# A windowed-attention network on one Trainium2 core: another order of TensorE's blocks in a slot

## The reference

```
def attn_layer(x, Wqkv, qs, ksc, Wo):          # x: 4 x 512 x 128, its second half of channels shifted by a token
    q, k, v = split(x @ Wqkv, 3)               # 1024 columns each
    q = rotary(l2norm(q) * qs)                 # with tables that depend on the position
    k = rotary(l2norm(k) * ksc)
    # a window of 32 queries sees its own 32 keys and the 32 before, masked to a band
    sim = einsum('bhwie,bhwje->bhwij', q, look_back(k)) * 8
    out = einsum('bhwij,bhwje->bhwie', softmax(sim), look_back(v))
    return out.reshape(b, n, 1024) @ Wo

def ffn_layer(x, g, bln, W1, b1, W2, b2):      # layer norm, 128 -> 2 x 341 -> 128
    a, gate = split(layernorm(x, g, bln) @ W1 + b1, 2)
    return a * gelu(gate) @ W2 + b2
```

## Time and profile before

| | |
|---|---|
| median of 3 runs | 1823.83 us (1823.41 to 1828.24) |
| the profiled execution | 1824.23 us, span 1822.2 us |
| granted TensorE clock, mean | 0.992 |
| PE busy | 1750.3 us, 96% |
| PEld busy | 1116.2 us, 61% |
| DVE busy | 1619.0 us, 89% |
| ACT busy | 1327.5 us, 73% |
| POOL busy | 1500.4 us, 82% |
| DMA | 16 engines 25.1% busy with the one queue |

### The profile page before, as it was taken

How to read it: one execution, slowest core, us unless ns; L and a number is a source line. 1 busy time by engine, 2 the same in 40 slices (tenths; PEclk the granted TensorE clock), 3 DMA queues, 4 the chain that set the end, 5 groups by cost and what they waited for, 6 DMA issues and landing times.

```text
span 1822.2 us, 48666 instructions
## 1 busy us (share of the span) xinstructions
PE 1750.3 (96%) x18122; PEld 1116.2 (61%) x18122; DVE 1619.0 (89%) x2782; ACT 1327.5 (73%) x2362; POOL 1500.4 (82%) x1204
## 2 busy tenths in 40 slices
PE   7699999999999999999999999999999999999986
PEld 6356666666666666666666666666666666666663
DVE  7799998999999989989999999899999998988874
ACT  3577877877778778778777777787776877877763
POOL 4799888888888888988888888888888888888860
PEclk9999999999999999999999999999999999999998
DMA  4132222222222222322223222222222222222221
GB/s 114 28 87 67 68 71 57 60 73 76 71 63 69 63 66 71 76 65 68 63 56 81 72 70 72 54 63 73 75 72 62 68 58 58 59 71 56 56 64 29
DMA packets 155273, 120.59 MB, mean 66 GB/s; under 512 B 42607, under 2 KB 151457, under 8 KB 154913
## 3 DMA queue, kind: packets, MB, share of 16 engines
q1 hardware_dynamic: 155041, 117.48, 25.1%
HBM read 18.79 MB, written 1.05 MB: 11 GB/s over the span
## 4 chain that ended last, share of the span: by engine, by line
PE 77%; DVE 13%; POOL 5%; issue 3%; SPq 1%; ACT 1%; DMA 1%; DVEq 0%; POOLq 0%; ACTq 0%
PE qk_bank L376 17%; PE ring_bank L448 10%; PE ring_bank L472 9%; PE ring_bank L389 8%; PE sc_bank L423 7%; PE ring_bank L516 6%; PE ring_bank L436 4%; PE ring_bank L399 3%; PE ring_bank L527 3%; PE ring_bank L461 3%; PE ring_bank L410 3%; DVE rn L842 2%; DVE step L837 2%; DVE o L898 2%; DVE qkn L858 2%
## 5 line engine op out<-in xcount | busy, mean ns | idle before, releaser
L1053 POOL TENSOR_TENSOR turned<-qkn,tables 128x512 f32<-128x512 f32 x384 | 489.3, 1274 | 209.8 <-DVE qkn L850 201.5
L1060 POOL TENSOR_TENSOR turned<-qkn,tables 128x512 f32<-128x512 f32 x384 | 496.7, 1294 | 0.0
L376 PE MATMUL qk_bank<-wqkv,xT 128*128 128x512 f32 x768 | 366.5, 600 | 18.8 <-DVE qkn L858 18.6
L1089 POOL TENSOR_TENSOR turned<-turned 128x512 f32<-128x512 f32 x192 | 255.0, 1328 | 15.1
L1096 POOL TENSOR_TENSOR turned<-turned 128x512 f32<-128x512 f32 x192 | 245.1, 1277 | 15.1
L448 PEld LDWEIGHTS ring_bank<-vw,pT 128*32 128x32 f32 x6144 | 156.6, 110 | 143.8 <-issue 143.7
L654 ACT ACTIVATE kB<-ring_bank 64x512 f32<-64x512 f32 x384 | 225.3, 587 | 23.5 <-PE ring_bank L410 21.2
L824 DVE TENSOR_REDUCE ss<-sq 128x16 f32<-128x1024 f32 x192 | 232.0, 1208 | 6.8 <-ACT sq L618 6.8
L627 ACT ACTIVATE vs<-ring_bank 128x512 f32<-128x512 f32 x192 | 114.7, 598 | 163.1 <-PE ring_bank L389 153.4
L898 DVE TENSOR_TENSOR o<-ring_bank,rr 128x512 f32<-128x512 f32 x192 | 132.1, 688 | 104.2 <-PE ring_bank L448 101.3
L389 PE MATMUL ring_bank<-wqkv,xT 128*128 128x512 f32 x384 | 216.1, 645 | 1.6 <-DVE x L978 1.6
(11 more groups left out here) (169 smaller groups left out, 3129.3 us busy)
## 6 DMA issues: line engine op xcount, KB each, us to landing
vw<-vs SPq DMA_DIRECT2D x1152, 64.0 KB, 2.1
vw<-vs SPq DMA_DIRECT2D x672, 32.0 KB, 1.9
wqkv<-in_L_ffn_Wqkv_dram SPq DMA_DIRECT2D x20, 384.0 KB, 3.5
wo<-in_L_ffn_Wo_dram SPq DMA_DIRECT2D x20, 128.0 KB, 3.3
w<-in_L_ffn_W_dram SPq DMA_DIRECT2D x6, 341.0 KB, 3.4
wqkv<-in_L_ffn_Wqkv_dram SPq DMA_DIRECT2D x1, 1536.0 KB, 9.5
x<-in_x_dram SPq DMA_DIRECT2D x2, 512.0 KB, 4.7
out_dram<-x SPq DMA_DIRECT2D x4, 256.0 KB, 2.3
```

Source lines behind the costliest of these rows:

```text
L376: mm = pe.matmul(QK[u % 2][:, i * UW:(i + 1) * UW], tok, wqkv[:, layer % 2, cut:cut + UW], start=True, stop=True)
L1053: return pool.tensor_tensor(heads(turned[:, u % 2, 2 * i, :]), heads(qkn[:, u % 2, i * UW:(i + 1) * UW]), table.unsqueeze(1).to_broadcast( ...
L1060: return pool.tensor_tensor(halves(turned[:, u % 2, 2 * i + 1, :]), halves(qkn[:, u % 2, i * UW:(i + 1) * UW])[:, :, ::-1, :], table.rearr ...
L1089: pool.tensor_tensor(q, q, turned[:, u % 2, 1, :], ALU.add).then_inc(q_summed, 1)
```

## The change

In PE's loop the v projection moves from behind attend to directly behind the q and k projections, and the turning of o moves behind the scores, so that attend and scores stand side by side. DVE's finish moves ahead of centre in the slots with s=1; it has work for the last four groups alone. The turns of the ring follow PE's order: v, pv, o, p in a slot where it was pv, v, o, p.

```diff
@@ PE's loop @@
             for n in range(SLOTS):
                 g, s = n // UPG, n % UPG
                 queries_keys(n)
+                values(n)
                 attend(n - 5)
-                values(n)
+                scores(n - 3)
                 transpose_o(n - 6)
-                scores(n - 3)
                 transpose_p(n - 4)
@@ DVE's loop @@
                 invert_sum(n - 5)
                 less_maxima(n - 4)
                 if s == 1:
+                    finish(g - 3)
                     centre(g - 2)
...
                 scale_o(n - 5)
                 if s == 3:
                     layer_norm(g - 2)
-                if s == 1:
-                    finish(g - 3)
```

## The result

The changed kernel takes 1871.97 us in the median (1871.19 to 1872.79, 4 runs) against 1823.62 for the kernel before: a ratio of 1.026, 95% interval 1.0242 to 1.0278, or 48 us slower. The profiled execution has a span of 1870.8 us.

What follows compares the result with a forecast made beforehand. PE was taken to bound most slots, with DVE needing 92% of the same time. Slot terms gave +1.11 a group, +24.4 over 22 groups, plus 1.4 for finish: 1824.23 becomes 1850, range 1812 to 1886.

Steps and rivals of the forecast that it cites:

- PE's saving: TensorE's slot: joining attend and scores leaves one tiling entry and exit of four, saving 0.37 us per slot.
- the 71 us: Upper limit of PE's saving: 0.37 in each of 192 slots, reached only if nothing else binds.
- DVE's loop and the lock: DVE: later attend delays scale_o; Newton steps wait for POOL products; slot 1 +0.26, slots 2 and 3 +0.95.
- the folded bias: PE work in slot 2 of one group in four, taking up most of the delay: 0.76 on average.
- ACT's chain: ACT runs oT, squares, pT; later o delays pT, holding q transposes: slot 0 +0.50, slot 4 +0.40.
- the four short slots: Slots 0, 1, 4 and 5 of a group, forecast at +0.50, +0.26, +0.40 and -0.27.
- Slots 6 and 7 are long ..., so PE's saving counts: ... -0.54: Slots 6 and 7: 19.53 less 2 x 0.37, plus 0.1 each for a bank held by oT: -0.54.
- 22 steady groups give +24.4: Whole run: the sum of +1.11 a group was counted over 22 steady groups, giving +24.4 us.
- the third rival: Lock missed in every slot: cycle 8.7 in slots 0, 1, 4, 5; +3.6 a group, 1903 us; chance 0.12.
- The first: Rival: DVE running ahead absorbs the longer loop, so only tiling savings count; 1753 or 1791 us; chance 0.14.
- The second: Rival: Newton steps of slots 2 and 3 slip through, pT costs half; 1828 us, within 0.3%; chance 0.10.
- If that cover goes, p waits for the v eviction some 0.2 a slot: ACT's v copy waits for later window DMAs; if later o stops covering this, p waits 0.2 a slot.

Runs made afterwards that it cites:

- both cuts and the seventh buffer: Changed kernel with ACT squaring before it copies o, POOL's q sum cut to 8 columns, and a seventh v buffer: 1781.82 us, ratio 0.9755.
- v_alone: Changed kernel with o put back ahead of the scores, so only v moves ahead of attend: 1867.2 us, ratio 1.0223.
- after_short_sum: Changed kernel with POOL's sum for q cut to 8 of 512 columns: 1821.61 us, 0.9969 of the kernel before.
- before_short_sum: Kernel before with POOL's sum for q cut to 8 of 512 columns: 1788.94 us, ratio 0.9791.
- join_early: Kernel before with the scores moved directly behind attend, ahead of v and o, attend staying in place: 1855.01 us, ratio 1.0151.
- o_alone: Kernel before with only the o transposes moved behind the scores: 1868.42 us, ratio 1.0232.
- squares_first: Changed kernel with ACT squaring q and k before it copies the turned o: 1869.74 us, ratio 1.0242.
- attend_first: Kernel before with attend moved ahead of the q and k projections: 1806.11 us, ratio 0.9891.

## Why the prediction was right

I forecast 1850 in a range of 1812 to 1886; 1872 lies in it, on the side and by the mechanism forecast, but the change cost 48 us and not 26. It stands at the very end of the forecast's own range of 1832 to 1872, so the mechanism was right and the size was not.

**PE's saving.** Forecast 0.37 a slot with the step from attend to scores at 0.83. It is 0.90 (929.82 - 928.92), so the step itself is 0.10, between its ends of 0.03 and 0.21 and nearer to the lower: the two blocks do join. The saving is 0.30 where nothing waits, as in slot 0 with both cuts and the seventh buffer (7.23 for 7.55). The cost of a change of tiling is there in the blocks (0.09 in, 0.18 out), as the drain that the Trainium skill (TensorEngine Tiling (Array Packing), Key Properties) gives to it would have it. But the 71 us were out of reach: 0.30 in 192 slots is 58, and even with three chains shortened the groups won 0.79 each and not 2.4.

**DVE's loop and the lock.** Right in place and size: scale_o forecast at 3.92, measured 3.92; slot 1 forecast at 8.4, measured 8.30; slots 2 and 3 +0.95, measured +1.02, and with the folded bias +0.76, measured +0.69 over groups 2 to 22. v_alone shows the cause, after_short_sum against before_short_sum the link through POOL's product. join_early shows that the link does not need a late attend. That the small DVE step and the POOL product exclude each other, as the Trainium skill says (SBUF — State Buffer, SBUF: two separate sides), fits the ends 0.04 apart and the 0.17 of the step without it.

**ACT's chain.** Slots 0 and 4 forecast at 8.05 and 7.95, measured 7.86 both. pT's end was forecast at 7.33 and measured at 7.31; the q transposes followed it by 0.06 where I had allowed more. o_alone and squares_first show the cause.

**What was mis-sized.** Over groups 2 to 22 the four short slots gave +0.94 (forecast +0.89) and slots 2 and 3 +0.69 (+0.76), so it was not there. Two terms were. First, "Slots 6 and 7 are long ..., so PE's saving counts: ... -0.54": they gave 0.18 in group 12. Slot 6 gave 0.20 and slot 7 nothing. The new order of turns puts attend's bank behind that of the output projection, so attend in slots 3 and 7 waits for the residual addition. In slot 7 (982.46) DVE ends it at 985.21, and attend starts at 985.32, 2.86 into the slot and not 2.67:

```profile
984.79 0.42 DVE L908 TENSOR_TENSOR xT<-xT,ring_bank 64x256 f32<-64x256 f32 x1
```

```profile
985.32 1.08 PE L448 MATMUL ring_bank<-vw,pT 128*32 128x128 f32 x32
986.19 1.08 PE L423 MATMUL sc_bank<-kB,qT 128*32 128x128 f32 x32
```

The join is dearer than taken, by 0.07 in slot 1 and 0.04 here (0.87 between the two rows), and the down projection, which waits for oT's bank, loses 0.15 in all where I had taken 0.1. Over the 21 groups these two slots miss the forecast by 7.7 us. Second, "22 steady groups give +24.4" left out groups 0 and 1. There the layer norm and the feed-forward blocks of PE are still missing, and the short slots run against DVE and POOL alone: in slots 0, 1, 4 and 5 of group 1 7.57 to 7.67 us each before and 8.66 to 8.95 after, which is the cycle of 8.7 that I had priced only for the third rival. Groups 0 and 1 give 8.2 us. The rest of the miss is the 5.3 us of the start, which I don't count as the change's since the same program starts at 52.60 too, and 2 us in group 23 and behind it.

**The rivals.** The first (only the changes of tiling count) is out: DVE ran behind, not ahead. The second (gains and losses cancel) is out too: in group 12 the third Newton step of slot 2 did not slip through (1.13 long), and over groups 2 to 22 slots 2 and 3 gave +0.69. The third was right about its cycle, but only in the short slots of the groups where those extras are missing. The fallback that I named in passing, "If that cover goes, p waits for the v eviction some 0.2 a slot", is in the profile (0.30 in slot 1), and it held slot 1 as soon as the other two chains were cut.

## What to carry to other kernels

When several engines run one software pipeline, moving blocks inside one engine's slot shifts when each block's reader is released. Price the shift for every reader, through its program order and back to the mover, before counting what the mover saves. An engine that is 98% busy can still gain by an order that releases its readers earlier, as attend_first shows, and lose by one that shortens its own work.

## What the runs showed of the hardware

- Two blocks of small matmuls in the same tiles (128*32), side by side, cost 0.90 for the first (0.87 in slots 3 and 7, where it had waited), one followed by full-array work 1.01, and full-array work behind it starts slower by 0.06 (transposes) to 0.10 (projections). Of the 0.30 a slot that joining saves, 0.11 is the exit, 0.09 the entry and 0.10 the slower work behind.
- A Newton step of 16 columns takes 0.17 alone and up to 1.30 beside a POOL product. Which product it meets moves by steps of a whole product: in slot 1 scale_o came 0.86 later and scale_k 0.16, in slot 2 scale_o 0.69 and scale_k 1.19.
- The first q/k matmul started at 51.3 to 52.9 us in nine of the thirteen profiles and at 55.9 to 57.2 in four, those with a granted clock at half for two thirds of the 15 us from 25 to 40.
